# Reordering rope steps, copies and low parts in a fused attention and FFN kernel on one Trainium2 core

## What is computed

```
q, k, v = layernorm(x) @ Wq, ctx @ Wk, ctx @ Wv
q = q * cos + rotate_half(q) * sin        # the rope
k = k * cos + rotate_half(k) * sin
scores = where(mask == 0, -1e9, q @ k.T / sqrt(128))
x = x + (softmax(scores) @ v) @ Wo
h = layernorm(x)
s = softmax(h @ router.T + router_bias);  w, idx = top_k(s, 8)
out = x + h * sum(w) + dense(w, idx) @ expert_bias
```

## Time and profile before

| | |
|---|---|
| median of 3 runs | 656.0 us (655.12 to 658.45) |
| the profiled execution | 656.07 us |
| its span in the trace | 654.3 us |
| PE busy | 598.5 us, 91% |
| DVE, POOL, ACT busy | 486.4, 417.2, 396.2 us |
| mean granted clock of PE | 0.965 |

### The profile page before, as it was taken

The page is one execution under the profiler, slowest core; times in us unless marked ns, Lnnn a source line. Parts: engine busy times, 40 slices in busy tenths (PEclk is TensorE's granted clock), DMA queues, the critical chain, the costliest instruction groups (busy, mean ns, idle before and its releaser), DMA issues.

```text
span 654.3 us, 10559 instructions
## 1 busy us (share of the span) xinstructions
PE 598.5 (91%) x2980; PEld 497.8 (76%) x2980; DVE 486.4 (74%) x796; ACT 396.2 (61%) x1054; POOL 417.2 (64%) x386
## 2 busy tenths in 40 slices
PE   9999896965799989999998999899989989999895
PEld 7888675744688878877887888788878878877673
DVE  5693899473688777958786887679677867886886
ACT  5245553454677667757666776577666756684453
POOL 5575857355687588866875875778668764365222
PEclk9999988997799999998999999899989998999998
DMA  8974242010310121130112101211211030100001
GB/s 291 347 212 140 65 146 81 33 33 1 113 49 18 49 81 50 48 82 14 64 48 80 48 16 48 80 48 48 50 46 64 0 97 2 34 17 1 34 32 67
DMA packets 30817, 45.40 MB, mean 69 GB/s; under 512 B 3008, under 2 KB 11328, under 8 KB 30784
## 3 DMA queue, kind: packets, MB, share of 16 engines
q1 hardware_dynamic: 30256, 43.95, 21.1%
q0 software_dynamic: 384, 1.05, 0.4%
q10 hardware_dynamic: 144, 0.00, 0.0%
HBM read 35.03 MB, written 9.96 MB: 69 GB/s over the span
## 4 chain that ended last, share of the span: by engine, by line
PE 32%; POOL 29%; issue 24%; DVE 8%; ACT 4%; POOLq 1%; DMA 0%; DVEq 0%; ACTq 0%
POOL w_lo L530 7%; POOL w_sum L497 6%; POOL probs L601 5%; POOL rot L486 5%; POOL wo_lo L491 4%; PE outp L1577 3%; PE score L1558 2%; PE outp L1579 2%; PE outp L1578 2%; DVE x_lo L1115 2%; PE bank_a L1430 2%; PE bank_a L1432 1%; PE bank_a L1431 1%; ACT probs L874 1%; DVE k_stage L1058 1%
## 5 line engine op out<-in xcount | busy, mean ns | idle before, releaser
L486 POOL TENSOR_TENSOR rot<-rot,sinT 128x512 f32<-128x512 f32 x80 | 110.5, 1381 | 62.8 <-ACT rot L725 62.6
L874 ACT ACTIVATE probs<-score,negmax 128x128 f32<-128x128 f32 x256 | 90.6, 367 | 61.1 <-DVE negmax L1203 61.1
L601 POOL TENSOR_TENSOR probs<-probs,rsum 128x512 f32<-128x512 f32 x64 | 67.5, 1055 | 70.9 <-DVE rsum L1209 70.9
L1577 PE MATMUL outp<-wo_hi,oT_hi 128*128 128x512 f32 x240 | 95.5, 398 | 2.0 <-DVE oT_lo L1228 1.3
L1579 PE MATMUL outp<-wo_hi,oT_lo 128*128 128x512 f32 x240 | 93.8, 391 | 0.0
L1578 PE MATMUL outp<-wo_lo,oT_hi 128*128 128x512 f32 x240 | 93.5, 389 | 0.0
L1216 DVE TENSOR_TENSOR resid<-resid,outp 128x512 f32<-128x512 f32 x60 | 41.1, 684 | 47.5 <-PE outp L1579 47.5
L1063 DVE TENSOR_TENSOR qT<-qT,rot 128x512 f32<-128x512 f32 x57 | 66.4, 1166 | 9.2 <-POOL rot L486 6.7
L1558 PEld LDWEIGHTS score<-kT,qT 128*128 128x128 f32 x512 | 69.1, 196 | 5.3
L1430 PE MATMUL bank_a<-x_hi,w_hi 128*128 128x512 f32 x128 | 56.5, 442 | 14.5 <-ACT part_t L754 5.8
L1558 PE MATMUL score<-kT,qT 128*128 128x128 f32 x512 | 69.3, 279 | 0.0
(11 more groups left out here) (273 smaller groups left out, 1534.2 us busy)
## 6 DMA issues: line engine op xcount, KB each, us to landing
ring_b<-in_wo SPq DMA_DIRECT2D x32, 256.0 KB, 2.6
ring_a<-in_wq SPq DMA_DIRECT2D x28, 256.0 KB, 2.8
v_dram<-v_stage SPq DMA_DIRECT2D x16, 256.0 KB, 3.9
v_raw<-v_dram SPq DMA_DIRECT2D x16, 256.0 KB, 2.6
k_dram<-k_stage SPq DMA_DIRECT2D x14, 256.0 KB, 2.0
kT<-k_dram SPq DMA_DIRECT2D x14, 256.0 KB, 2.7
ctx_in<-in_ctx SPq DMA_DIRECT2D x8, 256.0 KB, 4.2
ring_b<-in_wv SPq DMA_DIRECT2D x8, 256.0 KB, 7.1
```

Of the source, the lines that this page charges most:

```text
L486: pool.tensor_tensor(rot[:, k0 % 2, :], rot[:, k0 % 2, :], sinT[:, half * W:(half + 1) * W], ALU.mult).then_inc(sin_done, 1)
L601: pool.tensor_tensor(probs[:, p], probs[:, p], rsum[:, p, :].unsqueeze(2).broadcast_to([P, GH, S]), ALU.mult).then_inc(soft_done, 1)
L874: last = act.activation(probs[:, p, h, :], heads(score[p][:, :])[:, h, :], ACT.Exp, bias=negmax[:, p, h:h + 1], accum_out=sums[:, p, h:h + 1])
L1577: pe.matmul(ps[:, :], oT_hi[:, cols], w[0], start=h == 0, stop=False)
```

## The change

The change adds and removes no arithmetic. It moves instructions.

1. **Ropes of steps 0 and 1.** The rope of tile `hold` slot 4 (head 1, second half) was rope Q0+1, in step 1; it is now rope Q0, in step 0. The rope of the tile in `bank_a` (head 2, first half) was Q0, begun in step 0 and added in step 1; it is now Q0+1. On POOL both `rotate`s stay in step 0, but the first one now stands ahead of the four `lo_wo`. On DVE the add of the `bank_a` rope moves from between `mask_scores` and `row_max` to the end of step 1, behind `lo_p` and `accumulate`. On ACT the swap of slot 4 moves from step 1 to the start of step 0.
2. **Low parts of x.** Six of the seven of q = 0 are made in the last two turns of `copy_values`, one at k = 0; those of q = 1 at k = 5 to 11 (before: k = 0 to 6 and 7 to 13). ACT's high parts of q = 0 move ahead to match.
3. **Into the loop, ACT.** `hi_wo` moves ahead by two places each; `keep_t(2)` and `keep_u(2)` move ahead of `exps(0)` and `exps(1)`; `swap_c12(0, KK+5)` goes behind `exps(1)`; `hi_p` of step 0 ahead of a swap.
4. **Into the loop, DVE.** The four `wo_lo` are made two by two, all ahead of `make_c11(2)`, the first two ahead of rope KK+2. Ropes KK+5 and KK+6 move into step 0, behind `lo_p`. POOL's order ahead of the loop stays.

```diff
@@ pool, step
-            ROPE_HALF = (0, 1, 0, 0, 0, 1, 1, 1)
+            ROPE_HALF = (1, 0, 0, 0, 0, 1, 1, 1)
...
-                if last and b == 0:
-                    rotate((Q0, g, B), 1)
-                if b not in (0, 4) and not last:
+                if b == 0 or b not in (1, 4) and not last:
                     rotate((Q0 + b, g, B), ROPE_HALF[b])
                 if b == 0 and not first:
                     for h in range(GH):
...
-                if b in (0, 4) and not last:
-                    rotate((Q0 + b, g, B), ROPE_HALF[b])
+                if b == 0 and not last:
+                    rotate((Q0 + 1, g, B), ROPE_HALF[1])
+                if b == 4 and not last:
+                    rotate((Q0 + 4, g, B), ROPE_HALF[4])
@@ act, into the loop
             keep_s(0, 0)
+            hi_wo(0, 0)
+            hi_wo(0, 1)
             swap_c11(0, KK, 0)
...
             hi_w(W3, 2, 0)
+            hi_wo(0, 2)
+            hi_wo(0, 3)
             swap_c11(1, KK + 2, 0)
             keep_t(1, 0)
             hi_w(W1, 2, 0)
-            hi_wo(0, 0)
-            hi_wo(0, 1)
             keep_u(1, 0)
             hi_w(W2, 2, 0)
             swap_c21(1, KK + 3, 0)
-            hi_wo(0, 2)
-            hi_wo(0, 3)
             keep_s(2, 0)
             swap_c22(0, KK + 4, 0)
+            keep_t(2, 0)
             exps(0, 1, True)
-            keep_t(2, 0)
+            keep_u(2, 0)
+            exps(1, 2, True)
             swap_c12(0, KK + 5, 0)
             hi_w(W0, 3, 0)
             hi_w(W3, 3, 0)
-            exps(1, 2, True)
-            keep_u(2, 0)
             swap_c22(1, KK + 6, 0)
@@ act, step
-                if last and b == 0:
+                if first and b == 0:
+                    hi_p(n, True)
+                if b == 0:
                     swap_c12(1, Q0, g)
                 if not last:
-                    if b == 1:
-                        swap_c12(1, Q0 + b, g)
...
                 if b == 0 and not last:
-                    swap_c21(2, Q0, g)
+                    swap_c21(2, Q0 + 1, g)
@@ dve, values and keys
+                if i >= KB * B - 2:
+                    for j in range(3):
+                        lo_x(3 * (i - KB * B + 2) + j, 0)
...
-                if k < 7:
-                    lo_x(k, 0)
-                elif k < 14:
-                    lo_x(k - 7, 1)
+                if k == 0:
+                    lo_x(6, 0)
+                if 5 <= k < 12:
+                    lo_x(k - 5, 1)
@@ dve, step
                 if ahead:
                     mask_scores(b % 2, (b + FIRST) % B, n + FIRST + 1)
-                if not last and b == 1:
-                    add_rotated(Q0, g, B, hold[:, 3, :], qT[:, 0, 2, :])
...
                 lo_p(n, first and b == 0)
-                if last and b == 0:
-                    rope_query(hold[:, 4, :], 1, Q0, g, 1, 0)
-                    rope_query(None, 1, Q0, g, 1, 1)
-                if not last and b in ROPES:
+                if first and b == 0:
+                    rope_query(hold[:, 2, :], 0, KK + 5, 0, 1, 0)
+                    rope_query(None, 0, KK + 5, 0, 1, 1)
+                    rope_query(hold[:, 3, :], 3, KK + 6, 0, 1, 0)
+                    rope_query(None, 3, KK + 6, 0, 1, 1)
+                if b in ROPES and (b == 0 or not last):
...
+                if not last and b == 1:
+                    add_rotated(Q0 + 1, g, B, hold[:, 3, :], qT[:, 0, 2, :])
                 lo_o(n, first and b == 0)
```

More of the change, by code:

```diff
@@ L844, in _ @@
                     hi_w(W2, 1, 0)
-                if j in (4, 5, 6):
-                    hi_x((B11, B21, B22)[j - 4], 0)
+                if j == 4:
+                    hi_x(B11, 0)
+                    hi_x(B21, 0)
+                    hi_x(B22, 0)
                 if j == 6:
@@ L849, in _ @@
                     hi_x(T2, 0)
-                if j == 7:
                     hi_x(T3, 0)
@@ L943, in step @@
                         swap_c22(3, Q0 + b, g)
-                hi_p(n, first and b == 0)
+                if not (first and b == 0):
+                    hi_p(n, False)
                 if last and b == 0:
@@ L1228, in lo_o, with first_wo @@
                 dve.tensor_tensor(oT_lo[:, :], attnT[:, :], oT_hi[:, :].bitcast(F32), ALU.subtract).then_inc(ot_lo, 1)
+            def first_wo(h):
+                dve.wait_ge(b_hi, B_O + h + 1)
+                dve.tensor_tensor(wo_lo[:, h, :], ring_b[:, h, :], wo_hi[:, h, :].bitcast(F32), ALU.subtract).then_inc(b_lo, 1)
             for i in range(KS):
@@ L1240, in _ @@
             make_c11(1, 0)
+            for h in range(2):
+                first_wo(h)
             rope_query(hold[:, 3, :], 1, KK + 2, 0, 0, 0)
@@ L1246, in _ @@
             rope_query(None, 3, KK + 3, 0, 0, 1)
+            for h in range(2, GH):
+                first_wo(h)
             make_c11(2, 0, KK + 1)
-            for h in range(GH):
-                dve.wait_ge(b_hi, B_O + h + 1)
-                dve.tensor_tensor(wo_lo[:, h, :], ring_b[:, h, :], wo_hi[:, h, :].bitcast(F32), ALU.subtract).then_inc(b_lo, 1)
             mask_scores(0, 0, 1)
@@ L1257, in _ @@
             invert_sums(0, 1, True)
-            rope_query(hold[:, 2, :], 0, KK + 5, 0, 1, 0)
-            rope_query(None, 0, KK + 5, 0, 1, 1)
             invert_sums(1, 2, True)
-            rope_query(hold[:, 3, :], 3, KK + 6, 0, 1, 0)
-            rope_query(None, 3, KK + 6, 0, 1, 1)
-            ROPES = {1: (4, 1, 1), 2: (0, 0, 0), 3: (3, 1, 0), 5: (1, 2, 1), 6: (2, 0, 1), 7: (3, 3, 1)}
+            ROPES = {0: (4, 1, 1), 2: (0, 0, 0), 3: (3, 1, 0), 5: (1, 2, 1), 6: (2, 0, 1), 7: (3, 3, 1)}
             def step(g, b, first=False, lead=True, last=False):
@@ L1275, in step @@
                     if b == 2:
-                        dve.wait_ge(rope_done, Q0 + 1 + g * B)
+                        dve.wait_ge(rope_done, Q0 + 2 + g * B)
                         make_c11(3, g)
@@ L1280, in step @@
                     if b == 5:
-                        make_c12(3, g, Q0 + 2)
+                        make_c12(3, g, Q0 + 1)
                     if b == 6 and lead:
@@ L1310, in step @@
                         dve.wait_ge(proj_free, U_K + Q0 + g * B)
-                        times_cos(bank_a[:, :], Q0, g, B, hold[:, 3, :], 0)
+                        times_cos(bank_a[:, :], Q0 + 1, g, B, hold[:, 3, :], 0)
                     if b == 4:
                         times_cos(bank_a[:, :], Q0 + 4, g, B, qT[:, 0, 3, :], 0)
+                if not last and b == 1:
+                    add_rotated(Q0 + 1, g, B, hold[:, 3, :], qT[:, 0, 2, :])
                 lo_o(n, first and b == 0)
@@ L1545, in _, with scores @@
                                              ctxT_hi[:, c, cols], ctxT_lo[:, c, cols]) for c in range(C)]).then_inc(proj_done, 1)
-            def scores(b0, g, first=False, last=False):
+            def scores(b0, g, first=False):
                 p, b = b0 % 2, b0 % B
                 half, group = b // HB, b0 // B
-                pe.wait_ge(rope_done, KK + (half + 1) * GH + (half if not last else 0) + group * B + g * B)
+                pe.wait_ge(rope_done, KK + (half + 1) * GH + group * B + g * B)
                 if not first:
@@ L1583, in step @@
                 if not (last and b + FIRST >= B):
-                    scores(b + FIRST, g, last=last)
+                    scores(b + FIRST, g)
                 pe.wait_ge(soft_done, n + 1)
@@ L1595, in step @@
                     if b == 1:
-                        m1(3, g, U_K + Q0 + 1)
+                        m1(3, g, U_K + Q0 + 2)
                     if b == 2:
```

## The result

The changed kernel takes 630.18 us (median of 4 runs, 629.5 to 630.57). Beside it the kernel before took 657.23 (4 runs, 655.12 to 658.49). The ratio is 0.959, with a 95% interval of 0.9559 to 0.9622. The profiled execution took 630.11 us, at a mean granted clock of 0.98 (0.965 before).

What follows compares the result with a forecast made beforehand. PE, busy 91% of the span, was taken as the bound, held in the loop by six waits for pT_lo. Loop waits 13.4, clock 6.2, key stage 1.9 and entry 5.4 made 26.9 us off 656.07: forecast 629, range 627 to 632.

Steps and rivals of the forecast that it cites:

- What bounds the kernel: In the loop, PE's attnT waits for pT_lo, behind DVE's bank_a add held by POOL's sine, in groups 1 to 6.
- Loop, the waits: Step 1 of groups 1 to 6: PE's wait for pT_lo goes, 6 x 2.23 = 13.4 us.
- Loop, the clock: Loop: PE's clock drops after the wait, in 4 of 6 groups, go with it, 4 x 1.55 = 6.2 us.
- Rival (a): Loop: the waits go but the clock drops stay, made by something else; 635.4 us, chance 0.12.
- Moved steps at no cost: Loop, step 0: slot 4 swap, sine and DVE work (1.4 to 2.4 us) fit into idling of ACT, POOL and DVE.
- What is late next? I find nothing: Loop: no new wait follows; soften of step 0 ends near 355.4 and is wanted near 358.
- (e): Loop, step 0: slot 4 rope overfills DVE's 2.55 us idling and PE waits there instead; 641 us, chance 0.05.
- (f): Loop, step 0: slot 4 swap comes late, hi_p waits and PE stands at attnT in every group; 665 us, chance 0.03.
- Key stage: Six low parts of x moved early give 4.1 us, less 2.2 for half clock at m7: net 1.9, bounds 0 to 4.9.
- The port rule: Key stage: DVE and POOL take a shared port by whole instructions, so low parts meeting POOL's sums would gain nothing.
- rival (d): Port rule at its fullest on the way in: key stage gives 0, entry 4; 632.5 us, chance 0.08.
- Entry: From 141 us into the loop: m1 of step 1 starts at 167.1 instead of 172.48, gain 5.4 us.

Runs made afterwards that it cites:

- run 2: The changed kernel with DVE's add of the bank_a rope put back ahead of row_max in step 1: 652.98 us, ratio 0.9928 to the kernel before.
- run 1: The kernel before with one move: POOL's sine of the bank_a rope ahead of the four wo_lo; ACT and DVE stay: 641.97 us, ratio 0.9777.
- run 10: The changed kernel with the q = 1 low parts of x back at k = 7 to 13, those of q = 0 still early: 627.49 us, ratio 0.9557.
- run 5: The changed kernel with items 3 and 4 undone, except hi_p of step 0: 635.87 us, ratio 0.9676 to the kernel before.
- run 6: The changed kernel with DVE's ropes KK+5 and KK+6 ahead of lo_p in step 0 of group 0: 630.5 us, ratio 0.9586.
- run 7: The changed kernel with ACT's high parts of W1 and W2 (pair 3) moved behind the exponentials of step 0, hi_p ahead of them: 632.07 us, ratio 0.9609.
- run 8: The kernel of run 7 with rope KK+5 ahead of lo_p and KK+6 behind it on DVE: 631.95 us, ratio 0.9604 to the kernel before.
- run 9: The kernel of run 8 with POOL's sine of rope Q0 ahead of its low parts, the two hi_w behind the bank_a swap: 626.19 us, ratio 0.9538.
- run 12: The changed kernel timed once more, nothing altered, on the chip of another run: 630.3 us, ratio 0.9584 to the kernel before.
- run 4: The changed kernel with the low and high parts of x as before (item 2 undone): 630.44 us, ratio 0.9593 to the kernel before.

## Why the prediction was right, and where its sizes were off

629.0 was forecast, 630.18 measured.

- **What bounds the kernel.** Right. Run 2 shows it: in the changed kernel the add's place ahead of `row_max` is enough to bring back the wait of the earlier trace rows.
- **Loop, the waits: 13.4 forecast, 14.3 measured.** The step was right, the term too small by 0.15 us a wait: a stall costs 2.38 (59.66 less 57.28), not the 2.23 read between two matmuls in the earlier trace rows. PE's timeline has most of the rest: behind the wait the second matmul starts 0.34 us after the first (357.14 and 357.48), where 0.23 is usual.
- **Loop, the clock: 6.2 forecast, 6.1 left** (20.45 less 14.3). Rival (a), that the drops stay, is ruled out by the windows of the changed kernel and by run 2. The size is in part luck: four drops is the count of one execution, and run 2, with the same six waits, has five, at about 1.5 us each.
- **Moved steps at no cost.** Right, each with its cover: the slot 4 rope in DVE's idling (1.40 us, at the lower end of 1.4 to 2.4), its sine in POOL's. "What is late next? I find nothing" holds. Rivals (e) and (f) show in no group. What the slot 4 rope was moved for the forecast had not asked; run 1 answers with 6.6 us, by its trace.
- **Key stage: net 1.9 forecast, 0.4 measured.** This is the term that was mis-sized. `make_c11(0)` came at 115.05, 2.2 earlier, not 4.1. I had valued the six early low parts at 4.1, where run 10 shows 3.0. And I had put the q = 1 ones, moved two keys ahead, at nothing, where they take 0.8 back (114.23 against 115.05). The clock's cost at m7, 2.2 forecast, is 1.8 (2.22 gained at 117.81, 0.39 left at 137.70; run 10, without the low clock there, is at 123.46 while the changed kernel is at 125.87). The mechanism of the loss was as told; what I did not ask is whether one half of the edit could be had without it.
- **How firm these sizes are.** They come from one execution each. Eight traces here have this order of the low parts (this one and runs 2, 5 to 9 and 12), and from m7 to the same row they take 19.6 to 20.9 us, against 18.1 before: a cost of 1.6 to 2.9. The forecast's 2.2 lies in that range, so it was the gain, not the clock's cost, that it had wrong. All of these are differences between single traces, and executions with the same order so far differ by up to 0.8 us in when the key stage begins (first sine at 62.53 before and at 61.69 in run 1); the medians of run 10, run 4 and the changed kernel (627.49, 630.44 and 630.18) bear them out.
- **The port rule** of the Trainium skill ("SBUF — State Buffer", section "SBUF: two separate sides") as rival (d) gave 0 for the six. Where the two engines meet, the trace agrees with it, but only two of the six meet POOL's sums of x. Here are all six low parts (least, median and most, in ns), then POOL's first sum with the idle time ahead of it, the last two low parts, and two further sums:

```profile
L1117 DVE TENSOR_TENSOR x_lo<-x_raw,x_hi x6: 681/686/1777, 53.4 to 58.9; 128x512 fp32r<-128x512 f32 x6
...
57.08 1.33 POOL L561 TENSOR_TENSOR x_raw<-x_raw 128x512 f32<-128x512 f32 x1 [6.62 <-ACT x_raw L813]
57.18 3.48 DVE L1117 TENSOR_TENSOR x_lo<-x_raw,x_hi 128x512 fp32r<-128x512 f32 x2
58.49 1.61 POOL L563 TENSOR_TENSOR x_raw<-x_raw 128x512 f32<-128x512 f32 x1
60.07 1.74 POOL L564 TENSOR_TENSOR x_raw<-x_raw 128x512 f32<-128x512 f32 x1
```

Four take 0.68 us each, all begun while POOL idles, and two take 1.78 each beside the sums, of which two stretch from 1.29 and 1.31 us before to 1.61 and 1.74. POOL ends this work 0.75 us later (its first sine at 63.28 for 62.53), and 3 us are won. What failed in rival (d) for this stage is not the rule but its reach: most of the moved low parts ran where POOL stood idle.

- **Entry: 5.4 forecast, 5.15 measured** (5.55 less 0.4), and 5.7 by run 5. The walk held: first `soften` 147.98 for 147.7, POOL's sine of KK+5 150.14 for 150.0, `attnT` 159.64 for 160.5, m1 166.93 for 167.1 with a wait of 2.00 for 1.6. The slowed add was there too (160.29, 1.57 us, for the 1.73 put in).

Together 14.3 + 6.1 + 0.4 + 5.2 = 26.0. The loop gave 0.9 more than forecast, the way in 1.8 less.

## What to carry to other kernels

When an engine waits, look at what stands ahead of the late instruction in its own queue, and ask who needs that: here an add nobody needed soon stood ahead of `pT_lo`, and with the rest of the new order in place, that one instruction's place was worth some 22 us (run 2). Taking one wait away gains nothing where two more queues hold the next step nearly as long (runs 6 to 8), and the wait that moves takes the low clock behind it along (runs 7 and 8): walk them all and move the pieces together. And an idle stretch can be worth keeping where nothing hangs on it, if its removal puts the next one, and the low clock behind it, on the path.

## What was unexpected of the hardware

- A wait of 2.06 us on PE, between stretches in which it had been busy without a break, was followed by a drop to the lower clock level (1.2 GHz) in 4 of 6 groups before and in 5 of 6 in run 2, costing about 1.5 us each time, and not in the others, with the same wait and the same program around it. Whether it drops in one group or another I can't tell from these traces; the cause stays open. The six waits of run 1, 0.8 us at most, were followed by no drop at all.
- DVE and POOL slow each other both ways. DVE's low part of x goes from 678 ns to 1784 at most; POOL's weight sum from 0.72 to 1.17 us and its `probs` from 1.04 to 1.48 (run 6).
